# One block for the whole program: attention and a mixture of experts on one core, with the first loads moved ahead

## The reference

```
x = layernorm(x + attention(x))
x = layernorm(x + experts(x))

attention, 16 heads of 16 features, causal:
  q, k, v     = x@Wq, x@Wk, x@Wv
  q_amp       = softplus(q) / sqrt(mean(softplus(q)^2) + 1e-6)     (k_amp alike)
  q_phi       = pi * tanh(x@Wqp)                                   (k_phi alike)
  scores      = (q.k + lam*(q_amp cos q_phi . k_amp cos k_phi + q_amp sin q_phi . k_amp sin k_phi)) / 4
  out         = softmax(masked scores) @ v @ Wo

experts: 8 experts of width 512, the 2 best per token:
  gating = softmax(x@Wg + bg)
  e(x)   = silu((x@W1 + b1) * (x@W3 + b3)) @ W2 + b2
  out    = (sum of gate * e(x) over the two best) @ Wf + bf
```

## Time and profile before

| | us |
|---|---|
| runs | 2019.72, 2013.12, 2011.44 |
| median | 2013.12 |
| profiled execution | 2014.97 |
| its span, first to last instruction | 2013.3 |
| prepare, until DVE's last instruction | 234.1 |
| attend, PE's first to last matmul | 255.2 to 1325.6 |
| route, DVE's first division to POOL's last scatter | 1352.5 to 1500.6 |
| experts, PE's first to last matmul | 1512.1 to 1935.8 |
| finish, ACT's first instruction to the end | 1952.6 to 2013.3 |

### The profile page before, as it was taken

One profiled execution on the slowest core, in us unless ns is written; L12 is line 12 of the kernel. 1 busy time (PEld: TensorE's weight loads), 2 busy tenths in 40 slices (PEclk: granted clock), 3 DMA queues, 4 the chain that ended last, 5 costly groups with the idle time before them and its releaser, 6 DMA issues. The chain is left out here.

```text
span 2013.3 us, 28376 instructions
## 1 busy us (share of the span) xinstructions
PE 1736.0 (86%) x9130; PEld 917.9 (46%) x9131; DVE 1281.7 (64%) x3072; ACT 865.4 (43%) x1003; POOL 364.7 (18%) x487
## 2 busy tenths in 40 slices
PE   6999278999999999999999999946618999999956
PEld 3444133444444444444444444315514666666635
DVE  3588566777777777777777777207734555555537
ACT  1767513455545555555555555612301212212226
POOL 0111111111121111211112112111554111111111
PEclk9999667899999999999999999978659999999979
DMA  3455426002011020110201100037621111111134
GB/s 99 146 188 185 178 103 219 14 16 87 7 66 42 8 95 7 61 41 11 97 7 52 50 7 18 6 77 230 236 100 37 47 47 42 47 47 42 47 107 167
DMA packets 99498, 155.31 MB, mean 77 GB/s; under 512 B 10752, under 2 KB 60736, under 8 KB 99008
## 3 DMA queue, kind: packets, MB, share of 16 engines
q1 hardware_dynamic: 84928, 122.53, 18.6%
q0 software_dynamic: 14464, 31.40, 4.4%
HBM read 87.90 MB, written 65.35 MB: 76 GB/s over the span
## 5 line engine op out<-in xcount | busy, mean ns | idle before, releaser
L863 ACT ACTIVATE att_probs<-att_ps_s 128x1024 f32<-128x1024 f32 (+3 forms) x640 | 563.6, 895 | 520.4 <-PE att_ps_s L820 513.2
L820 PE MATMUL att_ps_s<-att_queries,att_keys 49*128 49x512 f32 (+3 forms) x2560 | 632.4, 562 | 20.0 <-ACT att_probs L863 11.4
L877 DVE TENSOR_REDUCE att_maxima<-att_ps_m 128x1 f32<-128x512 f32 x768 | 487.2, 683 | 156.1 <-PE att_ps_m L799 151.4
L799 PE MATMUL att_ps_m<-att_keys,att_queries 48*128 48x512 f32 (+3 forms) x1280 | 504.1, 607 | 48.5 <-DMA att_values<-v_rows 38.9
L799 PEld LDWEIGHTS att_ps_m<-att_keys,att_queries 48*128 48x128 f32 x1280 | 196.9, 193 | 339.6 <-DVE att_maxima L877 139.2
L880 DVE CUSTOM_DVE_ANT_0 att_ps_m<-att_ps_m,att_future 128x128 f32<-128x128 f32 (+3 forms) x512 | 240.2, 513 | 95.3 <-PE att_ps_m L799 94.0
L820 PEld LDWEIGHTS att_ps_s<-att_queries,att_keys 49*128 49x128 f32 x2560 | 242.0, 191 | 128.0 <-ACT att_probs L863 84.9
L839 PE MATMUL att_ps_o<-att_probs,att_values 128*32 128x512 f32 (+3 forms) x2560 | 269.4, 535 | 11.8 <-POOL att_probs L956 11.8
L1452 PE MATMUL exp_ps_h<-keep_w,exp_rows_t 128*128 x568 | 257.6, 596 | 5.4 <-DVE exp_rows_t L1483 5.4
L1525 ACT ACTIVATE exp_hidden<-exp_product 128x512 f32<-128x512 f32 x71 | 44.8, 630 | 320.6 <-DVE exp_product L1508 320.6
L956 POOL TENSOR_SCALAR_AFFINE_SELECT att_probs<-att_probs 128x512 f32<-128x512 f32 x128 | 81.1, 634 | 492.1 <-ACT att_probs L863 492.1
(11 more groups left out here) (189 smaller groups left out, 1486.7 us busy)
## 6 DMA issues: line engine op xcount, KB each, us to landing
att_queries<-q_parts SPq DMA_DIRECT2D x64, 192.0 KB
att_keys<-k_parts SPq DMA_DIRECT2D x64, 192.0 KB
exp_rows<-sorted_rows SPq DMA_DIRECT2D x71, 129.0 KB, 2.3
v_rows<-pre_v_sb SPq DMA_DIRECT2D x8, 1024.0 KB, 4.4
q_parts<-pre_waves SPq DMA_DIRECT2D x16, 512.0 KB, 3.1
k_parts<-pre_waves SPq DMA_DIRECT2D x16, 512.0 KB, 4.2
att_values<-v_rows SPq DMA_DIRECT2D x32, 256.0 KB
out_parts<-att_out_t POOLq DMA_DIRECT2D x32, 256.0 KB, 5.9
```

Of the source, the lines that this page charges most:

```text
L799: pe.matmul(take()[:, 0:width], queries[half, g % 2, c, r, P * q:P * q + P], keys[half, g % 2, k, r, 0:width], start=True, stop=True).then ...
L820: mm = pe.matmul(score_tile(unit, first, last)[:, e], keys[half, g % 2, k // TPC, r, P * (k % TPC):P * (k % TPC) + P].bitcast(F32), querie ...
L863: act.activation(probs[:, step % PROBS, DUO * r:DUO * r + DUO, first:last], score_tile(unit, first, last), ACT.Exp, scale=SCALE).then_inc( ...
L877: dve.tensor_reduce(to, buf[:, 0:width], AX.X, ALU.max).then_inc(s_mr, 1)
```

## The change

All five functions put their instructions into one block. Where an engine used to meet all others it now waits for the semaphores of what it needs. Tiles get fixed addresses through `Region`. The lower 40 KB (`EVEN`) belongs to even quads and is not used by `prepare`; `ODD` and the expert weights' place are shared with `prepare`'s tiles. The first quad (4 MB, 20 DMAs) is issued by SP in `prepare`, at the end of round 7. The three expert biases move from `route` to `attend` (issued after quad 6 is done), and `wo`, `wg`, `bias_g` move to the loads after quad 1. Identity and epsilon are made once. W2 keeps its four pieces in `route`.

```diff
+class Region:
+    def __init__(self, first, size):
+        self.next, self.last = first, first + size
+    def place(self, size):
+        at, self.next = self.next, self.next + -(-size // 32) * 32
+        assert self.next <= self.last
+        return at
...
 # prepare
-        block = stack.enter_context(nc.Block())
...
+            def load_first_quad(i, p):
+                if i == NCH - 1:
+                    sp.wait_ge(s_vout, 16 * QC)
+                    for kind in range(KINDS):
+                        for side in range(2):
+                            sp.wait_ge(s_out[kind][side], STORED * QC // 2)
+                    first_quad(sp)
...
                 (lambda i, p: store(i, 1, p), 3),
-                (lambda i, p: store(i, 2, p), 3)])
+                (lambda i, p: store(i, 2, p), 3),
+                (load_first_quad, 0)])
             sp.wait_ge(s_vout, 16 * NCH)
...
 # attend
+class Quads:
+    def load(self, sp, g):
+        for c in range(QC):
+            row, arrived = g // NQ * QC + c, self.loaded[g % 2][c]
+            for tile, rows in ((self.queries, self.rows_q), (self.keys, self.rows_k)):
+                for e in range(DUO):
+                    sp.dma_start(tile[g % 2][HALF * e:HALF * e + FEAT, c].rearrange("f r t -> f (r t)").bitcast(F32),
+                                 rows[row, DUO * (g % NQ) + e]).then_inc(arrived, 16)
+            sp.dma_start(self.values[g % 2][:, TPC * c:TPC * c + TPC],
+                         self.rows_v[row, :, :, g % NQ * QUAD * VW:(g % NQ + 1) * QUAD * VW]).then_inc(arrived, 16)
...
-            for g in range(QUADS):
+            for g in range(1, QUADS + 1):
                 if g >= 2:
                     sp.wait_ge(s_scores, (g - 1) * len(UNITS))
                     sp.wait_ge(s_pv, (g - 1) * STEPS)
...
+                if g < QUADS:
+                    quads.load(sp, g)
                 if g == 1:
                     for to, rows in first_weights:
                         sp.dma_start(to, rows).then_inc(s_expert, 16)
-            sp.wait_ge(s_expert, 16 * len(first_weights))
+                if g == QUADS:
+                    for to, rows in biases:
+                        sp.dma_start(to, rows).then_inc(s_bias, 16)
...
 # attend, tensor: instead of the constants' semaphore
+            pe.wait_ge(features.s_v, 2 * NCH)
+            pe.wait_ge(features.s_qk, 2 * NCH)
 # attend, gpsimd: ones under the keys of the odd buffer wait for the last stores of prepare
+                if i == 1:
+                    for kind in range(KINDS):
+                        for side in range(2):
+                            pool.wait_ge(features.s_out[kind][side], features.stored)
...
 # route, sync
-            sp.dma_start(wo[:, :], Wo.rearrange("(k p) n -> p k n", p=P)).then_inc(s_w, 16)
-            sp.dma_start(wg[:, :], Wg.rearrange("(k p) n -> p k n", p=P)).then_inc(s_w, 16)
-            sp.dma_start(bias_g[:, :], bg.partition_broadcast(P)).then_inc(s_w, 16)
+            sp.wait_ge(attended.s_pv, QUADS * STEPS)
             later = weight_blocks(w2, W2)
-            later += [(dst[:, :].rearrange("p e h -> p (e h)"), src.rearrange("e h -> (e h)").partition_broadcast(P))
-                      for dst, src in ((bias1, b1), (bias3, b3), (bias2, b2))]
...
+                last_quad = ((i // QC + 1) * NQ - 1) * QC + i % QC
+                sp.wait_ge(attended.s_store[last_quad % 2], 32 * (last_quad // 2 + 1))
+                sp.wait_ge(attended.s_kept[last_quad % 2], 16 * (last_quad // 2 + 1))
...
 # experts, sync
-            sp.dma_start(bias_f[:, :], bf.partition_broadcast(P)).then_inc(s_bf, 16)
+            sp.wait_ge(routed.s_tables, 1)
+            sp.wait_ge(routed.s_padded, 16 * NE)
+            sp.wait_ge(routed.s_put, routed.rows_put)
 # finish, sync
+            for p in range(4):
+                sp.wait_ge(mixed_rows.s_out[p], 16 * len(range(p, SLOT_TILES, 4)))
             sp.dma_start(wf[:, :], Wf.rearrange("(k p) n -> p k n", p=P)).then_inc(s_w, 16)
```

More of the change, by code:

```diff
@@ L14 @@
+from collections import namedtuple
 from contextlib import ExitStack
@@ L700, in attend @@
         n_ = Names(nc, stack, "att")
[L701 to L716, removed]
+        small, out_region = Region(ATT_SMALL, 4 * KB), Region(OUT_AT - 128, 4 * KB + 128)
+        ident, queries, keys, values, s_qkv = features.ident, quads.queries, quads.keys, quads.values, quads.loaded
+        probs = n_.sb(Region(PROBS_AT, 48 * KB), "probs", [P, PROBS, QUAD, CH])
+        future = n_.sb(small, "future", [P, CH])
+        max_row = n_.sb(small, "max_row", [QUAD * TPC, 2, P])
+        ones = n_.sb(small, "ones", [P, P // 2])
+        maxima = n_.sb(small, "maxima", [P, 2, QUAD * TPC, QC])
+        neg_max = n_.sb(small, "neg_max", [P, 2, QUAD * TPC])
+        sums = n_.sb(small, "sums", [P, 2, SUMS])
+        inverse = n_.sb(out_region, "inverse", [P, 2, SUMS])
+        out_t = n_.sb(out_region, "out_t", [P, 2, CH])
+        ps_m = [n_.ps(f"ps_m{i}", [P, CH]) for i in range(2)]
+        ps_s = [n_.ps("ps_s0", [P, DUO, CH])]
+        ps_m.append(n_.ps("ps_m2", [P, CH]))
         ps_o = n_.ps("ps_o", [P, CH])
+        ps_s.append(n_.ps("ps_s1", [P, DUO, CH]))
         s_made = n_.sem("constants_begun")
@@ new lines, in route @@
+        norm = Norm(n, small)
+        before = n.sb(small, "before", [P, P], BF16)
+        ones = n.sb(small, "ones", [P, P], BF16)
+        eps = n.sb(small, "eps", [P, 1])
+        gates = n.sb(small, "gates", [P, TPC, NE])
+        rest = n.sb(small, "rest", [P, TPC, NE])
+        top = n.sb(small, "top", [P, TPC])
+        same = n.sb(small, "same", [P, TPC, NE])
+        col = n.sb(small, "col", [P, TPC])
+        hot = n.sb(small, "hot", [P, 2, TOPK, TPC, NE])
+        chosen_place = n.sb(small, "chosen_place", [P, TOPK, TPC])
@@ new lines, in route @@
+        places = n.sb(small, "places", [P, TOPK, NT], U32)
+        both = n.sb(small, "both", [P, 2, TPC, NE], BF16)
+        place = n.sb(small, "place", [P, TPC, NE])
+        picked = n.sb(small, "picked", [P, TOPK, TPC, NE])
+        number = n.sb(small, "number", [P, NE])
+        starts = n.sb(small, "starts", [P, NE])
+        reached = n.sb(small, "reached", [P, NE])
+        pad_places = n.sb(small, "pad_places", [1, NE], I32)
+        count = n.sb(small, "count", [P, NE])
+        token = n.sb(small, "token", [P, NT])
```

371 lines of the change are left out of this document (187 added, 184 removed).

## The result

The changed kernel takes **1991.8 us** (median of 11 runs, 1987.8 to 2006.5) against 2018.4 (11 runs of the kernel before beside them, 2011.4 to 2026.9): ratio 0.988, 95% interval 0.986 to 0.991, so it is faster by 1.2%. The profiled execution has a span of 1987.5 us against 2013.3. The busy line hardly moved against the earlier trace rows: the same work, less idle time.

The account below looks back on a forecast made before the run. PE, busy 1736 of 2013 us, was taken to bound the kernel, leaving its 277 us idle to touch. Terms summed to -28.3 us from the profiled 2014.97, giving 1986.7, stated as 1986; range 1950 to 2003.

Parts of the forecast that it names:

- Seam prepare to attend: Start of attend: quad 0's early loads hold back stores that DVE waits for, so the first tile comes 12.2 us later.
- A: Start of attend: stores pass the early loads, which are free; seam -21.6 instead of +12.2 us, total 1953; chance 0.13.
- B: Start of attend: the loads hold only SP's issue, stores then land normally; seam -4.2 us, total 1970; chance 0.14.
- D: Start of attend: longer PE idleness keeps the clock at its lower level, +60 us, total 2046; chance 0.06.
- Seam attend to route: Between attend and route: SP issues route's first loads without the meeting, so DVE divides earlier; gain 15.1 us.
- Biases out of route: Route's last two long division rounds shrink to 11 us each without the 2 MB bias loads ahead; gain 10.2 us.
- Seams to experts and to finish: Before experts and before finish: loads or work start after the last landing without a meeting; gains 4.9 and 6.3 us.
- The end of the program: Last meeting, after finish: stays in both kernels, so no change in time was counted.
- rival C: Seams after attend, route and experts: empty stretches are needed for POOL's DMAs; 17.9 us of gain lost, 2005; chance 0.09.

Follow-up runs that it names:

- The loads last: Changed kernel with quad 0's 20 loads issued behind the last stores of prepare instead of in round 7; 1983.6 us, ratio 0.985.
- wide: Changed kernel with quad 0's queries and keys loaded at the same place by 12 transfers of outer dimension 16 instead of 16 of 3; 1983.3 us, ratio 0.984.
- spread: Changed kernel with quad 0's loads spread over prepare's rounds 5 to 8, five transfers behind each round's stores; 1970.5 us, ratio 0.978.
- spread behind x: Kernel with spread loads and GpSimd's drain moved, each chunk's loads issued one round later, behind the load of x; 1961.4 us, or 1954.4 with outer dimension 16.
- the kernel with the meetings back: Changed kernel with meetings of all engines put back behind attend, route and experts; 2013.0 us, ratio 1.000.
- the wide form spread over four rounds: Kernel with loads spread behind the load of x and drain moved, queries and keys by 12 transfers of outer dimension 16 per chunk; 1954.4 us, ratio 0.974.

## Why the prediction was right

Forecast were 1986 us and, term by term, 28.3 us off the profiled execution; measured were a median of 1991.8, 26.6 under that of the kernel before, and 25.8 between the profiles. What each term did is told below.

**Seam prepare to attend, right in sign, size and mechanism.** Forecast +12.2, measured +11.2; the profile behind the result showed the chain as told: a queue without gaps until 226.7, DVE idle 34.8 us where 33 were forecast, `abs_phase(7)` at 248.4 (249.4), first tile at 266.9 (268.0), no wait for chunk 1, the last 4 KB row of quad 0 at 239.4 (240). The loads last, wide, spread, and spread behind x moved the start to 252.4, 253.4, 245.2 and 234.0. Two details were wrong. The stores behind the loads do not only land late, they are issued slowly (5.08 and 2.45 us), and the price is not the three rings alone: with 16 it is still 19 us above a free start. By the rule for the number of engines in the Trainium skill ("DMA: Bandwidth & Descriptors", section "Why a DMA increments its semaphore by 16 and not by 1") the wide form uses all engines, and the share of 1.05 agrees; the rule says nothing of these being full too, nor of a 4 KB row taking three times as long.

**Rivals A and B fall** (DVE at 214 or 233; it was 248.4). **D falls:** the clock is at 0.61 in the stretch from 255 to 300, 0.79 from 330 to 370 (before: 0.61 and 0.74 in the same places of attend). After PE's restart at 267.3 the full level is back at 289.8, 22.5 us later; in the kernel before it took 19.2 (255.2 to 274.4), not the 17 of the prediction.

**Seam attend to route, right:** -14.6 for -15.1. The division comes 12.3 us after the end of the last matmul. I had said that POOL's constants do not decide. They do, by a hair: the copy of `token` at 1346.61 waits for POOL's last constant. POOL makes the constants behind its last store, which needs DVE's reciprocal, and this waits for a semaphore that two transfers raise: the sums landed at 1338.5, the output store only at 1344.1, 7.9 us after its issue beside the loads of `a_raw` (2.4 us in the kernel with the meetings back, where DVE idles 3.43 us instead of 8.95). The loads themselves had landed only 0.7 us before the copy, so the error is small.

**Biases out of route, right sign, mis-sized both ways.** The two rounds of the last divisions were 11.7 and 13.9 us, not 11 each: 6.6 us gained there (6.9 over all eight divisions) for 10.2. Then 6.4 us came behind the last division, where the kernel before has its unnamed waits; no run shows what they have to do with the change, so that the line of the table exceeds its forecast is luck. The experiments give the biases 5 to 8. Their new place in quad 7 cost nothing that shows.

**Seams to experts and to finish, right:** -6.6 for -4.9 and -5.5 for -6.3. In the first, the pads no longer land last: before, the last was issued at 1502.65, behind the last scatter, and now at 1469.20. SP issues the first rows at 1484.24, 0.8 us after the last landing (1483.44), as forecast.

**The end of the program, missed.** "The one meeting at the very end stays in both": it stays, but it costs 7.0 us instead of 1.2. The prediction put this term at nothing without looking at what the meetings did for GpSimd: its last drain was 0.7 us only because the meeting before finish had already drained it behind the 71 scatters. This is the part of rival C that was true: of 17.9 us of empty stretches 5.8 are owed at the end, unless the drain is put where GpSimd idles. The forecast sum of -28.3 against -25.8 measured is this, less what route gave more by its unnamed waits; that the two nearly cancel is luck, and the total is closer than its terms.

## What to carry to other kernels

A load issued early in a full queue is not early for what stands behind it: spread it over rounds with slack, behind the load that the next round needs; here that turned a loss of 11 us into a gain of nearly 22 at attend's start. When stages are joined, look for what each meeting paid in passing (here GpSimd's drain) and for who pays it now. And read a term of 5 us from its stretch, with the granted clock beside it before anything is called given back: two executions of the changed kernel, with clocks of 0.932 and 0.923, lie 17 us apart.

## What the runs showed of the hardware

- A GpSimd DRAIN took 6.8, 5.4, 5.9 and 0.7 us in the kernel before, behind 164, 65, 71 and 8 transfers that GpSimd had issued since the last one, and 6.5 us behind 308 at the end of the changed kernel. The number of transfers does not set it alone: counted from the end of the last issue, an early drain behind 300 took 5.9 us, as long as one behind 71. It is paid though all transfers have landed (at 1980.45, the drain runs from 1980.70 to 1987.22). Behind no transfer at all, at the end of prepare, GpSimd's drain took 4.14 us beside a product of its own of 4.04 us, so it waits for that as well.
- 768 rows of 4 KB took 0.17 us each in the mean when three engines loaded them, 0.50 us when 16 did at once (wholly busy, 128 GB/s), and 0.26 us in the wide form spread over four rounds; with 1 MB stores 0.88 of the engines moved 333 GB/s.
- A 512 KB transfer of a store, issued into rings that are full of loads, held SP 5.08 and 7.78 us, where 0.36 to 1.05 us is the rule.
- Attend took 1063.9 us with 78.7 us of it at the lower level of TensorE's granted clock, 1079.2 us with 105.1.
